# The bias of an attention output projection: as a product with a row of ones into PSUM, in place of additions on GpSimd

## What is computed

```python
x = x + tanh(g_xattn[0]) * xattn0(layernorm(x), ctx, ctx, group_prob, mask)   # 16 heads of 8 features
x = x + tanh(g_ffn[0])   * ffn0(layernorm(x))      # 8 experts, top 2, rows sent to the experts' slots
x = x + tanh(g_xattn[1]) * xattn1(layernorm(x), ctx, ctx, mask)
x = x + tanh(g_ffn[1])   * ffn1(layernorm(x))      # 8 experts, all computed, weighted by the top 2

def xattn0(q, k, v, group_prob, mask):
    q, k, v = q @ wq + bq, k @ wk + bk, v @ wv + bv           # then split into heads
    attn = softmax(q @ k.T / sqrt(8) + mask_term) * group_prob
    return (attn @ v, heads joined) @ wo + bo                 # bo: one row of 128 numbers
```

## Time and profile before

| | us |
|---|---|
| median of 3 runs | 1044.25 (1043.05 to 1044.91) |
| the profiled execution: its time | 1042.13 |
| the profiled execution: its span | 1040.3 |
| span of attention 0 with the sending of its rows | about 0 to 343 |
| experts 0 | about 343 to 496 |
| attention 1 | about 496 to 810 |
| experts 1 | about 810 to 1040 |

### The profile page before, as it was taken

The page is one execution under the profiler, slowest core; times in us unless marked ns, Lnnn a source line. Parts: engine busy times, 40 slices in busy tenths (PEclk is TensorE's granted clock), DMA queues, the critical chain, the costliest instruction groups (busy, mean ns, idle before and its releaser), DMA issues.

```text
span 1040.3 us, 20375 instructions
## 1 busy us (share of the span) xinstructions
PE 792.4 (76%) x6552; PEld 624.5 (60%) x6552; DVE 644.8 (62%) x1832; ACT 607.6 (58%) x2578; POOL 613.1 (59%) x978
## 2 busy tenths in 40 slices
PE   2278889878952699992125887778898789999997
PEld 1155667656741699992013665556676577888885
DVE  0267899988951222220245889999888656666664
ACT  1367988878830344440125888889998543444442
POOL 7454778887577100000688878976523267777775
PEclk9989999999975799996557999999999899999998
DMA  6848764666124122225143556654420000000000
GB/s 169 229 109 268 175 132 116 134 153 149 55 62 192 57 67 72 73 62 160 38 92 93 126 118 153 149 108 107 107 43 12 21 20 21 21 21 21 12 11 21
DMA packets 80067, 97.53 MB, mean 94 GB/s; under 512 B 7953, under 2 KB 67286, under 8 KB 79001
## 3 DMA queue, kind: packets, MB, share of 16 engines
q1 hardware_dynamic: 75864, 87.99, 32.9%
q0 software_dynamic: 4096, 8.25, 3.1%
HBM read 59.18 MB, written 41.58 MB: 97 GB/s over the span
## 4 chain that ended last, share of the span: by engine, by line
issue 26%; PE 25%; DVE 19%; POOL 15%; ACT 10%; DMA 3%; another core or an unknown queue 1%; SPq 0%; POOLq 0%; ACTq 0%; DVEq 0%
ACT exp L651 7%; PE psum L568 5%; PE psum L570 5%; PE psum L569 5%; DVE shift L814 5%; POOL got_rows L1219 3%; POOL scratch_xe L1201 2%; DVE exp_T L826 2%; PE psum L431 2%; POOL xn_rows L1139 2%; DVE ln_stats L796 1%; PE psum L445 1%; DVE inverse_spread L837 1%; POOL ln_rstd L1113 1%; PE psum L418 1%
## 5 line engine op out<-in xcount | busy, mean ns | idle before, releaser
L651 ACT ACTIVATE exp<-psum,shift 128x120 f32<-128x120 f32 x1024 | 366.2, 434 | 100.5 <-DVE shift L814 96.8
L651 ACT ACTIVATION_READ_ACCUMULATOR exp<-psum,shift 128x1 f32 x1024 | 273.8, 279 | 0.0
L814 DVE TENSOR_REDUCE shift<-psum 128x4 f32<-128x480 f32 x256 | 165.4, 646 | 73.4 <-PE psum L409 68.3
L418 PE MATMUL psum<-ident,exp 128*120 128x128 f32 x1024 | 163.2, 283 | 29.0 <-DVE exp_T L826 13.2
L1287 POOL TENSOR_TENSOR q_operand<-q_operand 128x512 f32<-128x512 f32 x96 | 125.9, 1312 | 69.9 <-DVE q_operand L1060 65.0
L1060 DVE SCALAR_TENSOR_TENSOR q_operand<-psum,comb,q_operand 128x256 f32<-128x256 f32 x256 | 111.6, 479 | 79.4 <-ACT q_operand L764 79.4
L764 ACT ACTIVATE q_operand<-psum 128x512 f32<-128x512 f32 x128 | 76.5, 599 | 122.0 <-PE psum L570 122.0
L418 PEld LDWEIGHTS psum<-ident,exp 128*120 128x120 f32 x1024 | 119.0, 142 | 47.2 <-DVE exp_T L826 17.1
L406 PE MATMUL psum<-neg_rows,const_bf 128*128 128x480 bf16 x256 | 99.8, 390 | 60.4 <-issue 20.2
L568 PE MATMUL psum<-w_T_high,xn_T_high 128*128 128x512 f32 x256 | 109.0, 426 | 9.9 <-DVE w_T_low L1026 7.4
L570 PE MATMUL psum<-w_T_high,xn_T_low 128*128 128x512 f32 x256 | 102.9, 402 | 0.0
(11 more groups left out here) (139 smaller groups left out, 1703.6 us busy)
## 6 DMA issues: line engine op xcount, KB each, us to landing
q_operand<-scratch_q SPq DMA_DIRECT2D x32, 384.0 KB
k_operand<-scratch_k SPq DMA_DIRECT2D x32, 360.0 KB
scratch_q<-parts SPq DMA_DIRECT2D x16, 384.0 KB
scratch_k<-parts SPq DMA_DIRECT2D x16, 360.0 KB
scratch_q<-parts SPq DMA_DIRECT2D x16, 256.0 KB
scratch_xe<-in_zero_rows SPq DMA_DIRECT2D x8, 512.0 KB, 11.3
scratch_k<-parts SPq DMA_DIRECT2D x16, 240.0 KB
xe_rows<-scratch_xe SPq DMA_DIRECT2D x16, 192.0 KB, 2.5
```

The costliest lines, as they stand in the source:

```text
L418: ins = pe.transpose(ps[0:S2, T_BANKS[G % 2], u * S:(u + 1) * S], atts[l].expS[:, G % RING_E, u, :], ident[:, :])
L651: ins = act.activation(atts[l].expS[:, G % RING_E, u, :], ps[:, S_BANKS[G % 3], u * S2:(u + 1) * S2], ACT.Exp, bias=atts[l].shift[:, i % 2 ...
L814: dve.tensor_reduce(atts[l].shift[:, i % 2, 4 * r:4 * r + 4], ps[:, S_BANKS[G % 3], 0:4 * S2].rearrange("p (h k) -> p h k", h=4), AX_X, AL ...
```

## The change

The bias is no longer added to x by POOL. PE puts it into the PSUM bank ahead of the projection: a product of a row of 128 ones (ones_row, one partition) with the row of bo (one partition, repeated four times, 512 columns) opens the bank, and the four products with wo add to it (start=False). DVE's L851 then multiplies the sum of both with tanh(g_xattn). POOL's 64 additions (L1169), DVE's two multiplications of bo (L1075) and DVE's wait for x_bias go; POOL's memset of the row of ones comes in at the start, and bo is loaded to one partition in place of 128.

```diff
 def out_project(l, c):            # PE
     C = l * NCH + c
     bank = misc(("o", C), x_new, C + 1)
+    on.wait_ge(const, 2)
+    pe.matmul(bank.rearrange("p (b d) -> p b d", b=CB), ones_row[:, :], bo[:, l:l + 1, :].broadcast_to([1, CB, D]), start=True, stop=False)
     on.wait_ge(o_T, CB * (C + 1))
     for b in range(CB):
-        ins = pe.matmul(bank[:, b * D:(b + 1) * D], atts[l].oT[:, (CB * c + b) % RING_O, :], wo[:, l, :], start=True, stop=True)
+        ins = pe.matmul(bank[:, b * D:(b + 1) * D], atts[l].oT[:, (CB * c + b) % RING_O, :], wo[:, l, :], start=False, stop=(b == CB - 1))
     ins.then_inc(mm_o, 1)
...
 def add_out(l, c):                # DVE
     on.wait_ge(mm_o, C + 1)
-    on.wait_ge(x_bias, CB * (C + 1))
     dve.scalar_tensor_tensor(xs, ps[:, bank_of[("o", C)], :].rearrange("p (b d) -> p b d", b=CB), tg_x[:, l:l + 1], xs, ALU.mult, ALU.add).then_inc(x_new, 1)
...
-        for l in range(2):
-            dve.tensor_scalar(bo[:, l, :], bo[:, l, :], tg_x[:, l:l + 1], None, ALU.mult).then_inc(bo_done, 1)
...
-        def add_bias(C):              # POOL
-            l, c = divmod(C, NCH)
-            on.wait_ge(ln_norm[0], CB * (C + 1))
-            on.wait_ge(bo_done, 2)
-            for b in range(CB):
-                pool.tensor_tensor(x[:, c * CB + b, :], x[:, c * CB + b, :], bo[:, l, :], ALU.add).then_inc(x_bias, 1)
...
-                    if o == at["bias"]:
-                        add_bias(C)
...
         pool.memset(half_c[:], -0.5).then_inc(const, 1)
+        pool.memset(ones_row[:], 1.0).then_inc(const, 1)
```

More of the change, by code:

```diff
@@ L91 @@
 NEAR = dict(k_project=0, k_take=1, k_part0=1, k_left0=1, k_part1=2, k_left1=2, k_out=(1, 2, 3), k_fetch=12,
-            stat=0, power=1, norm=3, turn=4, turned=5, bias=8,
+            stat=0, power=1, norm=3, turn=4, turned=5,
             q_project=5, q_take=6, q_part0=6, q_left0=6, q_part1=7, q_left1=7, q_out=(6, 7, 8), q_fetch=12)
 MID = dict(k_project=1, k_take=2, k_part0=3, k_left0=4, k_part1=4, k_left1=5, k_out=(6, 8, 10), k_fetch=16,
-           stat=0, power=1, norm=3, turn=7, turned=8, bias=9,
+           stat=0, power=1, norm=3, turn=7, turned=8,
            q_project=11, q_take=12, q_part0=13, q_left0=14, q_part1=14, q_left1=15, q_out=(16, 18, 20), q_fetch=22)
 FAR = dict(k_project=9, k_take=10, k_part0=11, k_left0=12, k_part1=12, k_left1=13, k_out=(14, 16, 18), k_fetch=22,
-           stat=0, power=1, norm=4, turn=11, turned=12, bias=13,
+           stat=0, power=1, norm=4, turn=11, turned=12,
            q_project=19, q_take=20, q_part0=21, q_left0=22, q_part1=22, q_left1=23, q_out=(24, 26, 28), q_fetch=30)
@@ L162, in flamingo @@
     bv = sb(top, "bv_rows", [S, 2, D])
-    bo = sb(top, "bo_rows", [S, 2, D])
+    bo = sb(top, "bo_row", [1, 2, D])
+    ones_row = sb(top, "ones_row", [1, 128])
     tg_x = sb(top, "tanh_g_xattn", [S, 2])
@@ L278, in flamingo @@
     spare_in = sem("spare_rows")
-    cols_done, tanh_done, bo_done, run0 = sem("cols"), sem("tanh"), sem("bo"), sem("r_run0")
+    cols_done, tanh_done, run0 = sem("cols"), sem("tanh"), sem("r_run0")
     ln_stats, ln_aggr, ln_pow, ln_rstd = sems("ln_stats", 2), sems("ln_aggr", 2), sems("ln_pow", 2), sems("ln_rstd", 2)
@@ L283, in flamingo @@
     mm_k, k_proj, k_part, k_left, k_out, k_in = sem("mm_k"), sem("k_proj"), sem("k_part"), sem("k_left"), sem("k_out"), sems("k_in", RING)
-    x_bias, mm_v, v_done = sem("x_bias"), sem("mm_v"), sem("v_rows")
+    mm_v, v_done = sem("mm_v"), sem("v_rows")
     mask_in, neg_done, group_in = sem("mask"), sem("neg"), sems("group", 2)
@@ L1305, in gpsimd_program @@
         left1(0, 0)
-        add_bias(0)
         attention(0)
@@ L1321, in gpsimd_program @@
         left1(0, NCH)
-        add_bias(NCH)
         for i in range(2 * CB, 3 * CB):
@@ L1505, in sync_program @@
             sp.dma_start(dst, src).then_inc(ld_first, 16)
-        for dst, src in ((g_in, t["g"].partition_broadcast(S)), (bo, t["bo"].partition_broadcast(S)), (wv, t["wv"]),
+        for dst, src in ((g_in, t["g"].partition_broadcast(S)), (bo, t["bo"].partition_broadcast(1)), (wv, t["wv"]),
                          (bv, t["bv"].partition_broadcast(S)), (cbf, t["cbf"]), (wo, t["wo"]), (iota8, t["iota8"]), (wg, t["wg"])):
```

## The result

| | before | after |
|---|---|---|
| median, us | 1044.91 (1043.05 to 1047.95, 5 runs) | 1053.6 (1052.14 to 1054.1, 5 runs) |
| the profiled execution: time, span | 1042.13, 1040.3 | 1052.14, 1050.3 |

The ratio is 1.0072, with a 95% interval from 1.0055 to 1.009. The change costs 8.7 us by the medians (7.5 by the ratio) where 3.7 were forecast, and the time lies above the range. The direction was right, and the size was off by a factor of two or more.

The account below looks back on a forecast made before the run. No engine was busy over 76%, so the chain of waits was taken as the bound. +7.7 - 0.6 - 1.3 - 0.45 - 1.65 = +3.7 on 1042.13 gives 1045.8, carried to the median 1047.9 us; range 1042 to 1052.

Parts of the forecast that it names:

- The price: PE's added fp32 one-row product: 0.86 us, scaled by width from L386's 0.81; bounds 0.21 and 1.12.
- Rival 1: PE's one-row product is cheap, 0.21 us like bfloat16: sum -2.7, 1041.5 us; chance 0.08.
- The nine places: Projections L445 on the chain of waits: eight at 0.86 us each, a ninth about 0.8, together +7.7 us.
- Rival 3: ACT absorbs the product at four places from 700 to 810 us: sum +0.3, 1044.6 us; chance 0.17.
- The last chunk: Projection of C = 15: one of seven places taken as covered, the product costed there at nothing.
- term (a): POOL's stretch, 153 to 209 us: two added products +1.7, long copy -1.1, PE's wait -1.2; term -0.6 us.
- Term (b): DVE's copy L837 at 219.24, 3.13 us long, ends up to 1.3 us earlier without the additions: -1.3 us.
- (c): Start of attention 1: additions at 525.34 stand ahead of POOL's L1111, DVE's L800 is next late; -0.45 us, not -1.73.
- (d): Additions at 567.68 directly ahead of POOL's normalisation L1139, for which PE waits 9.24 us: -1.65 us.
- Fewer long copies: Sign expected in the changed profile: DVE's copy L837 should have fewer long ones; no size given.
- Rival 2: POOL's stretch gives back its whole 3.4 us and the start of attention 1 1.73: sum -0.35, 1043.9 us; chance 0.15.
- Rival 4: All sixteen projections count, slack at covered ones used up: 13.8 less 4.0, +9.8, 1054 us; chance 0.10.

Follow-up runs that it names:

- the seven places: Changed kernel with the product only at C = 2, 3, 6, 7, 8, 9, 15, bias left out at the other nine: 1043.33 us, ratio 1.0006 to the kernel before.

## Why the prediction was wrong

**The price.** 0.86 us for the two instructions was right, and the nearer rows were the right ones: fp32 and 512 columns count, and the single row doesn't make it cheap. Rival 1 is dead by the row alone. What was missed is the 0.19 of the weights behind it. The step "0.81 x 512/480" took the row of L386, a product with 128 rows followed by one with 128 rows; there the next weights were loaded while it ran. Behind the single row they were not, and the price per place is 1.05.

**The nine places.** 8.25 us measured (2.7 either way) against 7.7 forecast. That this agrees so well is partly luck. With 1.05 each they would be 9.4, and one of them seemed not to count: at 704 us (C = 11) DVE's wait went from 1.35 to 1.26, and its addition moved by 0.1. The product was paid there by something else: DVE's operations between the additions of C = 10 and 11 took 4.2 us over their shortest time before the change and 2.5 after it. In the first kernel without bias, with 2.6 us of such excess, the distance of the two additions is 33.33 us, and in the changed kernel 34.39, a full price more. (These are single executions; the second one without bias has 32.80.) At the three behind it the waits are 2.89, 2.89 and 1.39 where before they were 1.84, 1.84 and 0.34. Rival 3, by which ACT absorbs these, fell: from C = 11 to 14 the additions move by 3.14 us, three full prices.

**The last chunk, which failed.** The prediction called it covered, together with the six others, since DVE has no wait there. That step looked at one engine only. The question at each place is also who waits for PE's next instruction, and behind this projection stand the products of experts 1. They had a cover too (PE's idle 1.09 and 2.90 us), which suffices at the upper level of the clock, as the trace of the seven places shows, and not at the lower. So it was costed at the wrong level of the clock; the prediction had named 1.7 us for a place with the clock down, and had not looked for which place that was. Cost: 1.6 us in the trace of the changed kernel and 1.7 in its second, 2.7 by the runs (not settled by their intervals), nothing where the clock was up.

**POOL's stretch, term (a), which failed by the most.** The prediction read 153 to 209 us of POOL in the chain, with 3.4 us of additions, and took from it two gains without the additions: 1.2 us, since PE waited for POOL once for 1.2 us, and 1.1 us of DVE's long copy at 189.08. The kernel without bias shows what is there without the additions: its additions to x at C = 1 and C = 4 come at 128.67 and 218.31 us, 89.64 apart, where before they were 88.60 apart (89.66 in the first run of the same kernel). Without the additions the stretch became 1.0 us longer, not 2.3 shorter. The traces show where. Of the three distances between additions, 29.43, 29.00 and 30.17 us before and 29.38, 29.98 and 30.28 without the bias, the first stayed. In the second an operation of DVE is now long that was not before, beside an operation of POOL:

```profile
175.48 1.15 POOL L1149 TENSOR_TENSOR full<-full,parts 128x512 f32<-128x512 f32 x1
175.52 1.13 DVE L891 TENSOR_SCALAR r_gate<-r_gate 128x4 f32<-128x4 f32 x1
```

It takes 0.15 us at its shortest, so 0.98 is added. In the third the copy of 189.08 is short, and the same L891 takes 1.37 us at 205.57 in its stead. With these lengthenings taken off, the second and third distances are 29.0 to 29.1 us in both kernels. So POOL's additions and PE's wait for POOL gave nothing there, and the long copy came back elsewhere. The chain of the changed kernel passes through this stretch by DVE's L817 and L827, ACT's L654 and DVE's waits for the projection, and no longer through POOL; POOL had been on it only because it was as late as the others (a reading). The products were not the error: each moved the next addition in full or nearly, 30.47, 30.80 and 30.80 us from one to the next in the changed kernel, so 1.1, 0.8 and 0.5 more than without the bias, 2.4 together where the prediction had 2.6. At +0.3 forecast and +3.5 measured, of which 3.3 is the gain that didn't come, this is the largest single part of the miss.

**The whole in two terms.** The prediction had 9.4 us of products (7.7, and 1.7 inside term (a)) and 5.7 given back. The runs have 12.4 of products (8.25 and 4.1) and 2.8 to 3.3 given back. So about half of the miss is what POOL's additions didn't give back, and half is the price of 1.05 and the places taken for covered. The intervals of the runs (2 to 3 us each) leave the halves uncertain.

**Term (b), the copy at 219.24.** It was forecast to end 1.3 us earlier. In the changed kernel no copy of DVE stands out there:

```profile
216.64 0.21 DVE L840 COPY inverse_spread<-inverse 128x128 f32<-128x128 f32 x1
...
225.54 0.21 DVE L840 COPY inverse_spread<-inverse 128x128 f32<-128x128 f32 x1
...
230.58 0.19 DVE L858 COPY r_logits<-psum 128x32 f32<-128x32 f32 x1 [2.27 <-remote]
```

The whole lengthening of 2.9 us is gone, so from C = 4 to 5 the change gained 1.9 us in spite of a product. The sign was right and the size too small. Before, the additions lay beside only the last 1.36 us of the copy; beside the rest lay POOL's L1201 (an indirect DMA, to 219.93) and L1162 (219.96 to 221.06).

**Terms (c) and (d).** -2.1 forecast, -2.6 measured. The detail of (c) holds: POOL's L1111 moved from 538.89 to 544.20, by 5.31, where the maxima at the start of attention 1 moved by 5.76, which is the 0.45 of the prediction. (d) is seen at the transposing of the third chunk, which waited 9.24 us before:

```profile
572.40 1.75 POOL L1139 TENSOR_SCALAR xn_rows<-x_rows,ln_rstd 128x128 f32<-128x128 f32 x4
...
574.29 1.09 PE L374 MATMUL psum<-ident,xn_rows 128*128 128x128 f32 x4 [7.41 <-POOL xn_rows L1139]
```

Its wait is 1.83 shorter. The kernel with product and additions both has 64.23 us from these maxima to the first addition, the kernel before 64.80, the changed one 62.24, which fits the additions as the cause.

**Part of what the additions gave back was lost again.** The prediction's last sentence named this as the way in which it would be wrong altogether: that the held-up operations of DVE move to other places. It happened between C = 9 and 10. DVE's small operations in the changed kernel, with what POOL does at that time:

```profile
655.30 1.50 DVE L931 SCALAR_TENSOR_TENSOR x_rows<-got_rows,slot_weight,x_rows 128x128 f32<-128x128 f32 x1
656.83 0.64 DVE L933 SCALAR_TENSOR_TENSOR x_rows<-got_rows,slot_weight,x_rows 128x128 f32<-128x128 f32 x1
...
657.60 0.98 DVE L916 SCALAR_TENSOR_TENSOR comb_sum<-comb_sum 128x4 f32<-128x4 f32 x1
...
659.37 2.15 DVE L925 TENSOR_TENSOR comb<-comb_work,comb_sum 128x32 f32<-128x32 f32 x1
...
661.65 0.65 DVE L817 TENSOR_REDUCE shift<-psum 128x4 f32<-128x480 f32 x1
```

```profile
658.96 1.19 POOL L1212 DMA_INDIRECT got_rows<-scratch_y,slot_get  x1 [0.16 <-issue]
660.18 1.27 POOL L1268 TENSOR_TENSOR w_T<-w_T,w_last 128x512 f32<-128x512 f32 x1
```

At their shortest, L931 takes 0.32 us, L916 0.16 and L925 0.19. Here they stand in a row ahead of one maxima of DVE, and ACT's exponentials behind it wait 4.39 us; before, at the same point of the program, they waited 1.58. The same 2.15 us stands in the kernel without bias (L922 at 653.78) and in the second execution of the changed kernel. The sum of all that DVE's operations take over the shortest of their line and form, for those that are over by more than 0.3 us, is 38.5 us before and 38.2 in the kernel with product and additions both; in the executions without the additions it is 33.8 to 36.7 (36.7 in the changed kernel). Taking 64 operations out of POOL's list lowered it by 2 to 5 us and for the rest moved it about. "Fewer long copies" is true of some places and false of others. How much of the kernel's loss from C = 8 to 10 (1.9 us, forecast at 0.8) is due to this and how much to the product at C = 10 no run here separates: the same kernel without bias took 68.57 us for this stretch in one execution and 72.90 in the other, where the kernel before took 69.01.

**Rival 2, POOL gives back more,** fell: the stretch gave nothing, and (c) gave its 0.45.

**Rival 1's sum** has an error of its own: with a product of 0.21 us the two in the stretch of term (a) save 2 x 0.65 = 1.3 us and not 0.6, so it should have read -3.4. It changes nothing here.

**Rival 4, all sixteen count (1054),** comes nearest in its number and had a chance of 0.10. The number is in part luck: its sum sets 4.0 us against the sixteen products, but the 4.0 already hold 1.7 for the two products in POOL's stretch, which are thus counted twice. Put right, it is 13.8 - 5.7 = 8.1, or 1052.3. As a mechanism it doesn't hold in the changed kernel: C = 6, 7 and 9 stayed covered (DVE has no wait at 6 and 9, and at 7 its wait went from 0.66 to 0.45 us). In the kernel with product and additions both (17.6 us) it isn't excluded by the time, but DVE has no wait at C = 6 there either.

**What stays open.** In the kernel after, the experts of block 0 and the sending before them take 1.1 us more, with nothing of the change in them, and DVE has waits that the profile puts down to "remote" alone, of 2.60, 1.98, 5.83 and 2.68 us before 231.67, 257.65, 305.13 and 328.68 us in the kernel before, and ones like them in the changed kernel (2.27 before 230.58, 2.69 before 262.45); at the first two PE and ACT stand still with it for 1.1 us, at the third for 3.1. No run was made for either. That a set of products costs 12 us over the kernel without bias and 17.6 over the kernel with the additions lies within what the intervals allow (4.4 and some 3 either way), so an interplay of the two was not shown.

## What to carry to other kernels

A product that adds a bias costs its type and its columns, not its rows. With 512 columns of fp32 it is 1.05 us of PE's time, and as three bfloat16 parts 0.32, which decided here between a loss of 0.7% and none. Before work is moved to PE, ask at each place what stands behind it in PE's own list and at which clock it will run, not only who waits for its result. Work of an engine that shares the chain with others at equal pace may give back nothing when it goes, and an operation that is held up beside it is no saving to be counted, since another may be held up in its stead. Run the kernel without that work first: the whole that can be gained (here 2.8 to 3.3 us of 27.6) is one run away.

## What the runs showed of the hardware that was not expected

Two products of one row in a row were followed by a fall of the granted clock, though PE was busy for 1.88 of 1.90 us in them. In the kernel with the product twice, the clock was at or near 1.00 ahead of the pair and lower in the 1.2 us before DVE's addition or the 3 us behind it at ten of the 16 chunks; at an eleventh (C = 7) it was low throughout. In the profiled execution of the changed kernel, with one product to a chunk, it stayed at 1.00 at 14 of 16; at C = 7 it fell while PE waited for o_T behind the product, and at C = 15 it had been low before. A second execution of it had a fall at C = 8 as well (0.68 ahead of the addition, 0.56 behind it), and three other kernels with one product had one behind C = 0 (0.52 to 0.54 in the 3 us behind the addition), where none of the kernels without a product there had. Why the clock falls behind the pair is not shown.

The weights of a product with 128 rows are not loaded while a product of one row runs: the loads stood idle for 0.76 us behind the weights of the fp32 product of one row and for 0.23 behind those of the bfloat16 one of three rows, and both times started again when the next product did. Behind a product of 128 rows the next weights of 128 rows were loaded while it ran, as in the eight of the projection.

A small operation of DVE takes several times its shortest time beside some operations of POOL: 1.13 us in place of 0.15 (L891 beside L1149), 2.15 in place of 0.19 (L925 beside L1212 and L1268). Beside the additions alone no such case was separated.
